# One core, three chained blocks in f32: a new order of the same operations and transfers on all engines

## What is computed

```
# 1. a transformer layer with a context of 2048 rows per batch
n = norm(x);  z = self_attn(n, Wq1, Wk1, Wv1);          y = ln(n + z)
z = cross_attn(y, context, Wq2, Wk2, Wv2);              y = ln(y + z)
z = relu(y @ fc1 + b1) @ fc2 + b2;                      x = x + ln(y + z)
# 2. an RWKV-7 mixing step; the two batches are its two time steps
n = norm(x);  r, w, k, v, a, g = (mix(n, mu_m) @ W_m for m in "rwkvag")
state update over two steps, group norm, bonus, gate;   h = ln(n + y * g @ Wo)
x = x + ln(silu(h @ Wf + bf))
# 3. attention with 8 heads and 5 experts, the best 2 of 5 for values and for outputs
n = norm(x);  q, k = n @ Wq, n @ Wk;  logits = n @ Ws, n @ Wd
v = sum_e gate_e * (n @ Wv_e);  p = softmax(q k^T / 8);  x = x + sum_e mask_e * (p v) @ Wo_e
```

## Time and profile before

| | |
|---|---|
| median of three runs | 247.75 us |
| the profiled execution, as a whole | 247.14 us |
| its span, first to last instruction | 245.4 us |
| PE busy | 226.6 us, 92% |
| DVE busy | 162.7 us, 66% |
| ACT, POOL busy | 92.8 and 75.5 us |
| moved by DMA | 43.99 MB |

### The profile page before, as it was taken

The page is one execution under the profiler, slowest core; times in us unless marked ns, Lnnn a source line. Parts: engine busy times, 40 slices in busy tenths (PEclk is TensorE's granted clock), DMA queues, the critical chain, the costliest instruction groups (busy, mean ns, idle before and its releaser), DMA issues.

```text
span 245.4 us, 3036 instructions
## 1 busy us (share of the span) xinstructions
PE 226.6 (92%) x1136; PEld 159.0 (65%) x1136; DVE 162.7 (66%) x314; ACT 92.8 (38%) x175; POOL 75.5 (31%) x74
## 2 busy tenths in 40 slices
PE   5899999999899999979988999999898689999994
PEld 5878778798688777648463444444343269799951
DVE  2036454757768995990481754989975769988971
ACT  2152041447278769402106226267501221322210
POOL 4052021106508652341140204375215314260000
PEclk9999999999799999999999999999999999999999
DMA  7999995069944977186600079940000000000001
GB/s 256 419 429 408 441 402 214 1 236 427 371 170 168 386 300 282 61 341 236 280 0 0 0 206 421 425 192 0 0 0 0 0 3 0 1 4 0 3 30 55
DMA packets 6351, 43.99 MB, mean 179 GB/s; under 512 B 832, under 2 KB 832, under 8 KB 1472
## 3 DMA queue, kind: packets, MB, share of 16 engines
q1 hardware_dynamic: 6336, 43.80, 44.9%
HBM read 43.27 MB, written 0.52 MB: 178 GB/s over the span
## 4 chain that ended last, share of the span: by engine, by line
PE 80%; DVE 9%; ACT 4%; issue 3%; POOL 2%; DVEq 0%; POOLq 0%
PE psum L398 76%; PE psum L402 4%; ACT slots L1440 3%; DVE small L817 2%; POOL small L1724 2%; DVE ring_r L841 1%; PE psum L515 1%; DVE slots_r L943 1%; ACT ring_r L1440 1%; DVE slots L835 1%; DVE slots L957 1%; DVE small L819 0%; DVE slots L825 0%; ACT slots_r L1440 0%; DVE small L821 0%
## 5 line engine op out<-in xcount | busy, mean ns | idle before, releaser
L398 PE MATMUL psum<-ring,slots 128*128 128x512 f32 (+3 forms) x228 | 90.5, 546 | 5.0 <-ACT slots L1440 5.0
L398 PEld LDWEIGHTS psum<-ring,slots 128*128 128x128 f32 (+1 forms) x228 | 39.4, 190 | 46.3 <-issue 35.4
L1440 ACT ACTIVATE slots<-psum 128x512 f32<-128x512 f32 (+3 forms) x43 | 22.8, 543 | 90.8 <-PE psum L398 51.1
L398 PE MATMUL psum<-slots,ring 128*128 128x128 f32 x448 | 52.7, 277 | 2.3 <-ACT slots L1440 2.3
L398 PEld LDWEIGHTS psum<-slots,ring 128*128 128x128 f32 x448 | 51.3, 192 | 4.2 <-ACT slots L1440 3.2
L398 PE MATMUL psum<-ring_r,slots_r 128*128 128x512 f32 x192 | 48.7, 407 | 1.7 <-DVE slots_r L943 1.7
L398 PEld LDWEIGHTS psum<-ring_r,slots_r 128*128 128x128 f32 x192 | 36.1, 194 | 11.6 <-DVE slots_r L943 2.6
L1729 POOL TENSOR_TENSOR ring_r<-ring,ring_r 128x640 fp32r<-128x640 f32 x16 | 30.8, 1934 | 36.1 <-ACT ring_r L1440 36.1
L1440 ACT ACTIVATE ring_r<-ring 128x2048 fp32r<-128x2048 f32 (+1 forms) x17 | 31.6, 1865 | 12.9 <-PE psum L398 8.3
L1724 POOL TENSOR_TENSOR small<-small,mhalf 128x1 f32<-128x1 f32 x16 | 12.7, 795 | 77.1 <-DVE small L821 77.1
L841 DVE TENSOR_TENSOR ring_r<-ring,ring_r 128x1408 fp32r<-128x1408 f32 x16 | 28.4, 1786 | 5.8 <-ACT ring_r L1440 5.8
(11 more groups left out here) (165 smaller groups left out, 205.0 us busy)
## 6 DMA issues: line engine op xcount, KB each, us to landing
ring<-blocks SPq DMA_DIRECT2D x36, 1024.0 KB, 8.3
bc<-vecs SPq DMA_DIRECT2D x1, 3072.0 KB, 28.6
bc<-vecs SPq DMA_DIRECT2D x1, 1280.0 KB, 7.0
slots<-xin SPq DMA_DIRECT2D x2, 256.0 KB, 6.1
bc<-vecs SPq DMA_DIRECT2D x1, 512.0 KB, 21.8
y<-slots SPq DMA_DIRECT2D x2, 256.0 KB, 2.0
colv<-cols SPq DMA_DIRECT2D x1, 14.0 KB, 7.1
```

The source lines that it names most:

```text
L398: return t.matmul(o_, l, r, start=first, stop=last)
L1440: return a.activation(o, x, func, **kw)
```

## The change

Every engine's list is permuted. No operation and no transfer is added, removed or resized; two names, `rt` and `gt`, are defined and not used. The lists of flag names (which say in which order a semaphore is counted up) follow the new order. The diff cut to its core (the lists of names are left out):

```diff
 SP
             eng.dma_start(X[0], xin[0, :, :]).then_inc(s_x[0], 16)
+            eng.dma_start(X[1], xin[1, :, :]).then_inc(s_x[1], 16)
             fetch("q1")
-            fetch("ct00")
             fetch("k1")
-            eng.dma_start(X[1], xin[1, :, :]).then_inc(s_x[1], 16)
+            fetch("ct02")
             fetch("v1")
...
+            fetch("ct13")
+            fetch("c01")
+            eng.dma_start(colv[:, :], cols).then_inc(s_cols, 16)
+            fetch("c02")
+            fetch("c00")
+            fetch("c12")
             fetch("c03")
+            fetch("c10")
             fetch("v2")
+            fetch("c11")
             fetch("c13")
+            fetch("ra")
             fetch("f1")
             s.wait_ge(*used("c11"))
             fetch("rf")
+            fetch("rv")
             s.wait_ge(*used("c13"))
             fetch("rw")
+            fetch("f2")
             fetch("rk")
+            fetch("fq")
...
 PE
             k1(0)
-            v1(0)
             turned_rows(1, "x", Y[1], 4)
             e1(0)
+            v1(0)
             count1(0)
...
+            scores(0, 2)
             scores(0, 1)
-            scores(0, 2)
...
             turn_p(1, 2)
+            turn_p(1, 3)
             s.wait_ge(*p_low[0].at("2"))
             v2(0)
-            turn_p(1, 3)
             gather(1, 1)
...
             step(1, "g", 5, 6, wait=rk_v[1].at("km"))
+            s.wait_ge(*rk_v[0].at("yg"))
+            transposes(bank(1), ys[0]).then_inc(*turn[0].inc("yg"))
+            ro(0)
+            s.wait_ge(*rk_v[1].at("yg"))
+            transposes(bank(5), ys[1]).then_inc(*turn[1].inc("yg"))
+            ro(1)
+            turned_rows(0, "h", hn[0], 3)
+            s.wait_ge(s_bc2, 16)
+            s.wait_ge(*rk_v[0].at("ys"))
+            bias("bf", 0)
+            rf(0)
...
             bias("bf", 4)
...
+            fk(1)
+            turn_p0(0)
             fq(1)
+            av(0, 0)
             score_f(1, 1)
             score_f(1, 0)
-            av(0, 0)
+            turn_p0(1)
+            score_t(1)
+            turn_max(1)
             av(0, 1)
-            turn_max(1)
-            score_t(1)
             less_max(1)
-            sum_u(0, 0)
             av(1, 0)
             av(1, 1)
+            sum_u(0, 0)
...
 DVE
             start(0)
+            start(1)
             norm(0, "x", Y[0], X[0])
-            start(1)
...
+            p_split(1, 2)
+            low("c12")
+            add2(0)
+            norm2(0)
+            s.wait_ge(s_cols, 16)
+            v.tensor_scalar(rest, colv[:, 0:24], -1.0, 1.0, ALU.mult, ALU.add).then_inc(*rest_v.inc("rest"))
+            p_split(1, 3)
+            low("c13")
             weigh2(1)
-            low("c11")
-            low("c12")
+            done2(0)
             row_low("a0")
-            add2(0)
-            p_split(1, 2)
-            norm2(0)
-            low("c13")
-            p_split(1, 3)
...
             norm_h(1)
+            silu(0)
             affine(1, "h", hn[1], TMP[1], "norm_b")
-            silu(0)
             out_s(0)
...
 ACT
             silu(0)
-            select()
             copy_turned(1, "h", T10, 7)
...
+            fk_out(1)
             fq_out(1)
-            fk_out(1)
-            p0_turned()
+            select()
             max_turned(1)
...
 POOL
-            expert(0, 3, vv[0]).then_inc(*own_g.inc())
...
+            expert(1, 3, vv[1]).then_inc(*own_g.inc())
             s.wait_ge(*prod[1].at("w"))
             g.memset(sel, 0.0).then_inc(*own_g.inc())
...
-            expert(1, 3, vv[1]).then_inc(*own_g.inc())
+            s.wait_ge(*prod[0].at("g"))
+            s.wait_ge(*prod[1].at("g"))
+            g.memset(VV[1][:, :, 64:65], 1.0).then_inc(*exp_g[1].inc("ones"))
             expert(1, 4, vt2[1]).then_inc(*own_g.inc())
```

More of the change, by code:

```diff
@@ L171, in build @@
         kt = [slot(R[b][0]) for b in range(2)]
+        rt = [slot(R[b][1]) for b in range(2)]
         vt = [slot(36), slot(R[1][2])]
@@ L174, in build @@
         km = [slot(2), slot(R[1][4])]
+        gt = [slot(R[b][5]) for b in range(2)]
         ys = [slot(R[b][6]) for b in range(2)]
@@ L741, in _ @@
             step(0, "a", 0, 1, bias_of="a0")
+            step(0, "k", 1, 2)
+            s.wait_ge(*y_in[1].at("3"))
+            bias("w0", 7)
             s.wait_ge(*p_low[1].at("3"))
@@ L744, in _ @@
             bias("a0", 6)
-            step(0, "k", 1, 2)
-            s.wait_ge(*y_in[1].at("3"))
-            bias("w0", 7)
             turned_rows(1, "n4", N4[1], 4)
@@ L750, in _ @@
             step(1, "k", 0, 5, wait=evict[1].at("relu"))
+            step(0, "r", 3, 0, wait=turned[0].at("n4"))
             step(1, "a", 1, 6, bias_of="a0")
-            step(0, "r", 3, 0, wait=turned[0].at("n4"))
             step(1, "w", 2, 7, bias_of="w0")
@@ L1203, in _ @@
             masked(1)
+            low("ct00")
+            pT(1)
+            low("ct01")
+            k2_split(0)
             weigh(1)
-            low("ct02")
-            pT(1)
-            k2_split(0)
             add1(1)
@@ L1405, in _ @@
             expert(1, 0, True)
-            max_f(0, 1)
             expert(1, 1, False)
-            p0_turned()
             expert(1, 2, False)
+            out_gate(0, 0)
+            gate_out(0, 0, 0)
             max_f(1, 1)
@@ L1833, in _ @@
             g.memset(VV[0][:, :, 64:65], 1.0).then_inc(*exp_g[0].inc("ones"))
-            deviation(1, "h")
+            expert(0, 4, vt2[0]).then_inc(*own_g.inc())
+            expert(0, 3, vv[0]).then_inc(*own_g.inc())
+            s.wait_ge(*own_g.now())
+            g.tensor_tensor(vv[0], vv[0], vt2[0], ALU.add).then_inc(*exp_g[0].inc("vv"))
+            expert(1, 3, vv[1]).then_inc(*own_g.inc())
             s.wait_ge(*prod[1].at("w"))
```

368 lines of the change are left out of this document (167 added, 201 removed).

## The result

The new order is slower: 254.53 us (median of four, 253.09 to 255.26) against 247.77 (247.38 to 247.85), a ratio of 1.027 (95% interval 1.022 to 1.032). The prediction was 247.2, with a range up to 249.5. The profiled execution of after took 253.09 us, its span is 251.4, 6.0 above that of before.

A forecast was written before the change was run, and what follows sets the result against it. PE was taken to bound the kernel, busy 226.6 of 245.4 us. The terms sum to -0.6 us: from the profiled 247.14 that gives 246.5, and with the median 0.6 above, 247.15, say 247.2; range 245.6 to 249.5.

The forecast's parts named there:

- Start: From the start through the first products: reordered norms, v1 and e1 summed to +0.2 us, bounds 0 and +0.7.
- First scores: At PE's first scores: scores(0, 2), now first, waits for DVE's k2_split; +0.7 us.
- Context blocks: Fetches of context blocks in another order, some much later: they land in time for ACT and DVE, no cost.
- Rival 1: Behind the shut-out of batch 0: the clock doesn't fall, 1.5 us less, 245.7 us; chance 0.14.
- Last gathers: At the last gathers: PE's waits for p_split(1, 2) and p_split(1, 3) go; -2.0 us, bounds -2.3 and 0.
- f2: Fetch needed 8.4 us after the last gather, now second behind the wait for c13; +0.1 us, bounds 0 and +0.3.
- Block 2 and the bias: Block 2: products up to 174 us unchanged, bounds 0 and +1.5; bias("bf", 4) leaves PE's path, -0.43 us.
- silu ahead of the affine: Norms at block 2's end: affine(1, "h") now stands between silu(0) and out_s(0) in the critical chain; +0.55 us.
- Attention: Block 3: av(1, 0) loses sum_u(0, 0), which covered ACT's exponential; +0.3 us, bounds +0.1 and +0.4.
- rival 2: Block 3: DVE late for turn_max(1), PE waits 1.8 and 0.4 us, 2.2 us more, 249.4 us; chance 0.22.
- its last sentence: Sign against the forecast: a half clock elsewhere, above all between 188 and 196 us, where PE has 3.6 us nearly idle.

The follow-up runs named there:

- e11: The kernel of e3 with 22 matmuls on constants between the transpose of x(0) and q1(0), filling PE's wait for q1; ratio to before 1.013.
- e3: The kernel before with one edit, X[1] fetched as the second transfer instead of the fifth; ratio to before 1.022.
- e4: The kernel after with four more products on constants ahead of turn_max(1) on PE; 251.26 us, ratio to before 1.022.
- e17: The kernel after with the start as before and, on DVE, the maxima of batch 1 ahead of out_gate(0, 0) and gate_out(0, 0, 0); 247.3 us, ratio 1.001.
- e5: The kernel after with the start as before (X[1] behind three blocks, old order of v1, e1 and the norms); 250.9 us, ratio 1.015.
- e13: The kernel after with DVE's maxima of batch 1 and p0_turned() ahead of out_gate(0, 0) and gate_out(0, 0, 0), run again for its trace; 247.7 and 252.5 us.
- e8: The kernel before with only the order of the last gathers changed (DVE's p_split calls earlier, turn_p(1, 3) ahead of v2(0) on PE); ratio 0.995.
- e14: The kernel of e13 with PE's list of block 3 as before and p0_turned() ahead of expert(1, 1) on DVE; 263.7 us, ratio 1.066.
- middle alone: The kernel after with start and block 3 as before; ratio to before 0.987, and 0.993 (245.27 us) when repeated on another chip.
- three runs with mends on the middle alone: The middle alone with ct01 first, ct13 ahead of c00 and f2 earlier (1.001); without the ct01 edit (1.001); or with affine(1, "h") ahead of silu(0) (0.997).

## Why the prediction was wrong

The forecast of -0.6 us was a sum of waits, and those that it named were mostly right. Step by step:

- Start, +0.2 (bounds 0 and 0.7): +2.9. Two terms were wrong. The step took X[1]'s transfer as one that matters to DVE alone, and did not ask what the second transfer does to the third: q1, wanted at 7.8, landed at 8.8, +1.1 us. And a wait of 2 us ahead of the first products was not held against the clock: +1.5. (Of seven traces with such a wait, 1.25 to 2.8 us and not filled, six have slow first products; but so have five of the eleven with the wait of 0.69. Only e11 against e3 speaks for the wait as the cause.) The wait of 0.44 for `k1_out` was as written (0.45), and the one for the count of row 0 went.
- First scores, +0.7: +0.8, with `k2_split` as the cause.
- Context blocks, nothing: PE waited 0.99 us for POOL's low part of ct13. The step went through ACT and DVE for c03 to c13; POOL's list and ct13 were left out. (Its 83.5 for c03 is also a slip: 76 + 4.7 + 2.5 is 83.2. Nothing hangs on it.) On ACT ct13's split stands behind c00's, whose block landed late (ACT waited 1.59 us for it at 73.75).
- Rival 1, no half clock behind the shut-out, had 0.14. It came true: 24 matmuls in 5.76 us against 7.28 in the earlier trace rows, -1.5. The argument against it, that nothing shortens the low stretch, was about the wrong quantity: the stretch ahead of it had changed, its wait going from 0.99 to 0.57 us.
- Last gathers, -2.0: -2.3, the lower bound. f2, +0.1 (up to 0.3): a wait of 0.44, in place of another.
- Block 2 and the bias, -0.43 in all: from n4(0) to yg(0) the trace has -1.15. The bias row is right; of the rest 0.43 are two bias rows that run together (below), and 0.3 I can't place.
- silu ahead of the affine, +0.55: +0.5; turned h(1) waited 1.65 us where 1.8 stood, and n5(0) 0.87.
- Attention, +0.3: +5.4. Here rival 2 (0.22) had the mechanism, DVE late for `turn_max(1)` by products that POOL holds, and it happened: 0.80 and 0.32 us where 1.8 and 0.4 stood. Its price, 2.2 us, left out what follows: the clock at a half for 10.2 us, in which PE is busy throughout. At half pace `less_max`, av(1) and the first sums cost 0.9, 1.8 and 2.0 us more than in the trace of before.

Two terms failed, the start and the attention, which held no wait for q1 and none ahead of `turn_max(1)`. But the missed waits, some 2 us with the delay that they bring, are the smaller part: what failed most is what a wait is worth. The earlier trace rows was in the text as the place where the clock fell, and gave the rival that it might go. The same row should have been read as a price to hold against every new wait: behind a stretch in which PE stands for one microsecond or more, 1.5 to 5 us can follow that no list shows. The prediction looked for such a place in its last sentence, between 188 and 196 us, and gave it no price; the two that decided were the start and 226 us. e4 and e11 show it by filling the wait, e17 against e5 by ending it. It is a risk and no rule: behind the wait of 1.25 us in e13 the clock held, and it fell behind waits of 0.33 us in e4, e13 and e17 and behind none in e3.

Left open: what makes one wait bring the clock down and a like one not, and whether PE's own order in block 3 adds to it. Near 67 us the clock fell in all five profiles with a wait of 0.95 to 1.18 us ahead of the shut-out, not in e8 with 0.89, and in one of thirteen with 0.57 (e14). Between h and n5 the same lists fell in one profile and held in another.

## What to carry to other kernels

- A wait of the bottleneck engine has two prices, its length and the slow clock behind it; here the second was up to four times the first. Read the granted clock beside every wait; here the dearest new wait stood among small matmuls.
- A new order is a hundred small changes that add up only where nothing is shared. Try it by stages: its middle alone was 0.7 to 1.3% faster than before, and two places, mended by a few moved lines, cost 2.6%; the rest of its block 3 took back what the middle gains.
- If a mend takes out a wait, look at what stands in its shadow. None of the three runs with mends on the middle alone was faster than it.

## What was not expected of the hardware

- A transfer of 256 KB as the second in the queue makes the 1 MB behind it land 6.7 to 8.2 us after its issue (eight traces) instead of 4.8 to 5.6 (the other eleven). Why is not shown.
- The pace at the start is a matter of the execution: with the same wait of 0.69 us ahead the first 64 matmuls took 7.4 to 7.5 us in five profiles and 9.2 to 9.4 in five others (in e8 a transfer came between), and kernels with the same lists did both. The Trainium skill ("TensorE: Matmul & The Clock Gate", What's actually happening) says that the number of slow matmuls at a start varies from run to run; the traces agree.
- Two bias rows on 64 partitions take 0.42 us together when they stand side by side, and 0.43 each when they stand apart (142.16 and 138.10 in the trace of before):

```profile
142.68 0.50 PE L400 MATMUL psum<-bc_r,share 64*128 64x512 f32 x2
143.10 0.66 PE L404 MATMUL psum<-ident,slots 128*128 128x128 f32 x4
```

The Trainium skill ("TensorE: Matmul & The Clock Gate", Why this matters for your kernels) says that matmuls of few partitions run at the same time where they lie in different row groups; `a0` stands in partitions 0 to 63 and `w0` in 64 to 127 (line 207 of the kernel after), which fits, but no run here moved them to the same ones.
